# Row maxima 28 tiles ahead instead of 26 in a 16-head attention, and another way of fetching the bias scale before it

## The reference, cut to what matters

```
xn   = layernorm(x)
q, k, v = split(xn @ W_qkv.T)                    # 16 heads of 16, per batch 2048 tokens
core = -dist / max(dist) * 0.1                   # 256 points; dist = pairwise distance of the centres
bias = zeros(N, N); bias[1:257, 1:257] = core
attn = softmax(q @ k.T * scale + bias)
s    = (attn @ v) @ W_proj.T + b_proj + layernorm(xn)
out  = x + s * silu(ffn(xn))
```

## Time and profile before

| what | value |
|---|---|
| median of 3 runs | 2928.17 us |
| profiled execution: its own time | 2928.38 us |
| profiled execution: span of the core | 2926.6 us |
| mean granted TensorE clock | 0.993 |
| PE busy | 2883.0 us (99%) |
| DVE busy | 2336.9 us (80%) |
| ACT busy | 2222.5 us (76%) |
| POOL busy | 1265.3 us (43%) |

### The profile page before, as it was taken

One profiled execution on the slowest core, in us unless ns is written; L12 is line 12 of the kernel. 1 busy time (PEld: TensorE's weight loads), 2 busy tenths in 40 slices (PEclk: granted clock), 3 DMA queues, 4 the chain that ended last, 5 costly groups with the idle time before them and its releaser, 6 DMA issues.

```text
span 2926.6 us, 107289 instructions
## 1 busy us (share of the span) xinstructions
PE 2883.0 (99%) x44160; PEld 2025.9 (69%) x44160; DVE 2336.9 (80%) x4346; ACT 2222.5 (76%) x4251; POOL 1265.3 (43%) x2348
## 2 busy tenths in 40 slices
PE   8899999999999999999999999999999999999998
PEld 4467666655667755767657777777777777777776
DVE  7899999999999999999856776777677677767765
ACT  4599999999999999999966666666666666666664
POOL 5432333333333323332345455555555554555554
PEclk9899999999999999999999999999999999999999
DMA  7631111111111111111121111111111111111110
GB/s 233 211 115 41 49 49 45 43 49 49 41 46 49 49 39 48 49 49 39 44 65 45 36 31 37 40 47 44 30 37 33 47 45 36 31 38 39 47 43 5
DMA packets 157393, 154.78 MB, mean 53 GB/s; under 512 B 17794, under 2 KB 130946, under 8 KB 156930
## 3 DMA queue, kind: packets, MB, share of 16 engines
q1 hardware_dynamic: 156930, 148.15, 16.3%
HBM read 89.37 MB, written 58.72 MB: 51 GB/s over the span
## 4 chain that ended last, share of the span: by engine, by line
PE 95%; DVE 2%; POOL 1%; ACT 1%; issue 1%; SPq 0%; DMA 0%; POOLq 0%; DVEq 0%; ACTq 0%
PE banks L1534 29%; PE banks L1492 15%; PE banks L1460 15%; PE banks L1475 14%; PE banks L1601 4%; PE banks L1549 4%; PE banks L1639 4%; PE banks L1568 3%; PE banks L1616 2%; PE banks L1429 1%; PE banks L1626 1%; DVE pair_max L1145 1%; PE banks L1447 1%; POOL row_max L641 1%; PE banks L1714 0%
## 5 line engine op out<-in xcount | busy, mean ns | idle before, releaser
L1145 DVE TENSOR_REDUCE pair_max<-banks 128x1 f32<-128x1024 f32 x1024 | 1212.4, 1214 | 106.9 <-PE banks L1460 76.4
L919 ACT ACTIVATE probs<-banks 128x512 f32<-128x512 f32 x2048 | 1186.5, 599 | 99.3 <-PE banks L1475 13.1
L1475 PE MATMUL banks<-q_aug,k_aug 98*32 98x512 bf16 x8192 | 845.7, 381 | 0.2
L1460 PE MATMUL banks<-k_aug,q_aug 96*32 96x512 bf16 x8192 | 663.0, 383 | 8.5 <-DVE pair_max L1145 3.8
L1492 PE MATMUL banks<-probs,v_cur 128*32 128x256 f32 x8192 | 655.7, 379 | 2.1 <-POOL probs L635 2.0
L1492 PEld LDWEIGHTS banks<-probs,v_cur 128*32 128x32 f32 x8192 | 319.3, 111 | 144.1 <-issue 2.4
L1460 PEld LDWEIGHTS banks<-k_aug,q_aug 96*32 96x32 bf16 x8192 | 276.8, 97 | 188.2 <-DVE pair_max L1145 60.2
L641 POOL TENSOR_SCALAR row_max<-pair_max 128x1 f32<-128x1 f32 x508 | 139.6, 278 | 611.0 <-DVE pair_max L1145 603.1
L1475 PEld LDWEIGHTS banks<-q_aug,k_aug 98*32 98x32 bf16 x8192 | 287.3, 95 | 150.4 <-ACT probs L919 4.7
L1534 PEld LDWEIGHTS banks<-hnT,w_sb 128*64 128x64 f32 (+1 forms) x5632 | 308.5, 137 | 25.1 <-ACT hnT L998 25.1
L1534 PE MATMUL banks<-hnT,w_sb 128*64 128x128 f32 (+1 forms) x5632 | 323.9, 275 | 0.9 <-ACT hnT L998 0.9
(11 more groups left out here) (143 smaller groups left out, 4020.5 us busy)
## 6 DMA issues: line engine op xcount, KB each, us to landing
acc_scratch<-acc_sb SPq DMA_DIRECT2D x128, 256.0 KB, 2.5
heads_win<-acc_scratch SPq DMA_DIRECT2D x512, 64.0 KB
q_aug<-q_parts SPq DMA_DIRECT2D x192, 64.0 KB, 2.2
k_aug<-k_parts SPq DMA_DIRECT2D x192, 64.0 KB, 2.2
q_parts<-parts SPq DMA_DIRECT2D x16, 384.0 KB, 3.1
k_parts<-parts SPq DMA_DIRECT2D x16, 384.0 KB, 4.1
x_in<-in_x SPq DMA_DIRECT2D x10, 512.0 KB, 4.9
xT_scratch<-xnT SPq DMA_DIRECT2D x8, 512.0 KB, 5.4
```

Of the source, the lines that this page charges most:

```text
L919: nc.scalar.activation(probs[:, step % PRING, :], banks[:, ring(h, step), :], ACT.Exp, scale=SCALE).then_inc(prob_ready, 1)
L1145: nc.vector.tensor_reduce(pair_max[:, group % 2, q, half:half + 1], banks[:, 4 + 2 * (t % 2):6 + 2 * (t % 2), :], AX.XY, ALU.max).then_inc ...
L1460: last = nc.tensor.matmul(banks[m:m + CT, 4 + t % 4, :], q_aug[0:TERM_ROWS, b, q * P + m:q * P + m + CT], k_aug[0:TERM_ROWS, b, kq * BANK: ...
L1475: last = nc.tensor.matmul(banks[m:m + CT, ring(h, step), :], k_aug[0:AUG, b, kb * P + m:kb * P + m + CT], q_aug[0:AUG, b, qc * CHUNK:(qc + ...
```

## The change

`LEAD` goes from KB + 10 to KB + 12, for TensorE and VectorE alike. The maximum over partitions goes by DRAM: SyncE stores one value per partition, waits for it, and loads all 128 into every partition; VectorE reduces them. In chunk 7 VectorE does the distances' sum ahead of `split_rest(c, 0)` and their maximum ahead of `split_rest(c, 2)`. TensorE waits for `v_saved` after the first pair of max tiles instead of ahead of it. The first three score steps stand after 22, 24 and 26 max tiles, where the first stood after 26.

```diff
-LEAD = KB + 10
+LEAD = KB + 12
+EARLY = SRING
@@ sync, behind the loop over chunks
+            sp.wait_ge(dist_red, 1)
+            sp.dma_start(dmax_dram, dmax[:, 0:1]).then_inc(dmax_stored, 16)
+            sp.wait_ge(dmax_stored, 16)
+            sp.dma_start(dmax_all[:], dmax_dram.rearrange("p o -> (p o)").partition_broadcast(P)).then_inc(dmax_in, 16)
             for mb in range(NMB):
                 sp.wait_ge(parts_stored[mb], 16 * (NCHUNK + 1))
             load_aug(0, 1)
@@ gpsimd, chunk 7
-                if not ahead2 and not ahead:
-                    pool.wait_ge(dist_red, 1)
-                    nc.gpsimd.partition_all_reduce(dmax[:, 1:2], dmax[:, 0:1], P, RMAX).then_inc(dist_red, 1)
@@ vector
-                split_rest(c, 0)
-                residual(c, u)
                 if not ahead:
                     dve.wait_ge(dist_step, 3)
                     nc.vector.tensor_tensor(dist[:], dist[:], dtmp[:], ALU.add).then_inc(dist_step, 2)
+                split_rest(c, 0)
+                residual(c, u)
                 split_rest(c, 1)
+                if not ahead:
+                    dve.wait_ge(dist_sqrt, 1)
+                    nc.vector.tensor_reduce(dmax[:, 0:1], dist[:], AX.XY, ALU.max).then_inc(dist_red, 1)
...
-                if not ahead:
-                    dve.wait_ge(dist_sqrt, 1)
-                    nc.vector.tensor_reduce(dmax[:, 0:1], dist[:], AX.XY, ALU.max).then_inc(dist_red, 1)
                 split_rest(c, 3)
@@ vector, behind turn_shift(0, 0)
+            dve.wait_ge(dmax_in, 16)
+            nc.vector.tensor_reduce(dmax[:, 1:2], dmax_all[:], AX.X, ALU.max).then_inc(dist_red, 1)
             dve.wait_ge(dist_red, 2)
@@ tensor
-            pe.wait_ge(v_saved, NCHUNK + 1)
...
-            for t in range(LEAD):
+            for t in range(LEAD - 2 * EARLY):
+                if t == 2:
+                    pe.wait_ge(v_saved, NCHUNK + 1)
                 max_tile(0, t)
             pe.wait_ge(minus_set, 1)
+            for step in range(EARLY):
+                scores_to_exp(0, step)
+                for t in range(LEAD + 2 * (step - EARLY), LEAD + 2 * (step - EARLY) + 2):
+                    max_tile(0, t)
...
-                    if not (ends and step >= STEPS):
+                    if not (ends and step >= STEPS or h == 0 and step < EARLY):
                         scores_to_exp(h, step)
```

More of the change, by code:

```diff
@@ L13 @@
 AX = mybir.AxisListType
-RMAX = bass.bass_isa.ReduceOp.max
 BANK = 512
@@ L95, in build @@
     res_dram = nc.dram_tensor("res_scratch", (T, D), F32, kind="Internal").ap()
+    dmax_dram = nc.dram_tensor("dmax_scratch", (P, 1), F32, kind="Internal").ap()
     acc_dram = nc.dram_tensor("acc_scratch", (B, HEADS, P, N), F32, kind="Internal").ap()
@@ L134, in build @@
         dmax = sb("dmax", [P, 8], F32)
+        dmax_all = sb("dmax_all", [P, P], F32)
         v_all = sb("v_all", [P, T // P, D], F32)
@@ L220, in build @@
         dist_red = sem("dist_red")
+        dmax_stored = sem("dmax_stored")
+        dmax_in = sem("dmax_in")
         dist_scale = sem("dist_scale")
```

## The result

The changed kernel takes 2948.36 us, the median of 6 runs (2946.18 to 2950.89); the kernel before took 2928.25 us in 6 runs beside it. The ratio is 1.0069, interval 1.0056 to 1.0082: slower by 20.1 us, where 15.3 us were forecast. Its profiled execution took 2948.12 us at a span of 2946.3 us and a mean granted clock of 0.994.

A forecast was written before the change was run, and what follows sets the result against it. TensorE was taken to set the pace in the middle of stage 2, VectorE at its start. Start -4.3 and lead +19.6 us: 2928.2 - 4.3 + 19.6 = 2943.5 us, range 2938 to 2955.

The forecast's parts named there:

- The lead: Stage 2, step 75 of 15 heads: TensorE's stall grows from 0.29 to 1.60 us, 15 x 1.31 = +19.6 us.
- the chain: Each head with a next: step 71's weighted call, GpSimd's copy, row maxima, VectorE's turn of group 5's shift; 2.08 us.
- Rival A: Step 75: the hold does not grow with the lead, so only the start counts, 2923.9 us; chance 0.10.
- Rival B, the clock: Stage 2: the 1.6 us stall drops the granted clock, 1.7 us a head, 2956 to 2969 us; chance 0.09.
- Group 1's cover of 0.9 us: Each head: group 1's turn, behind batch 0's bias factors, stays covered, taken as 0; if not, 0 to 4 us.
- The switch of GpSimd's code: Start of stage 2: GpSimd's 5.4 us before the bias factors is the switch back from the reduction's code, and goes.
- rival C: Start of stage 2: GpSimd's 5.4 us stays, the start gains about 0.5 us, total 2947.3 us; chance 0.06.
- The start: Start of stage 2: earlier pairs and bias factors bring pair 20 at about 135.05; together -4.3 us.
- I take the store as landed at 116, the broadcast at 119: Bias scale at the start: SyncE's store and broadcast of the maxima finish then, so VectorE, asking at 119.8, needn't wait.
- My bound of -2.6: The start's smallest gain, -2.6 us, with a late broadcast; the other bound was -5.5.
- SyncE's queue: Start: the wait and two issues put the 12 loads back about 1 us, `phase1_end` 122.2 to 123.2; covered.
- the room above the forecast: Range's upper end, 2955 us: group 1 adds its 4 us and some heads lose the clock.

The follow-up runs named there:

- second run: Kernel before with only the lead changed from 26 to 28, its old start kept: 2950.43 us, ratio 1.0073.
- run 12: Changed kernel with a lead of 30 tiles instead of 28: 2994.65 us, ratio 1.0228.
- run 9: Changed kernel with group 5's maxima ahead of GpSimd's copy and the maximum over partitions by TensorE, plus an unused store of 128 neighbouring 4-byte values: 2918.78 us.
- runs 10 and 11: As run 9, but the unused store writes its values 512 bytes apart, or 128 full rows of 512 bytes: 2918.05 and 2918.45 us.
- runs 5 and 6: Changed kernel with group 5's maxima ahead of GpSimd's copy and the maximum over partitions by TensorE, leads 28 and 26: 2918.68 and 2917.26 us.
- run 7: Changed kernel with the 4-byte store of the maxima issued earlier, behind the first store of the q parts: 2944.94 us, ratio 1.0053.
- run 4: Kernel before (lead 26, old start) with group 5's maxima and shift ahead of GpSimd's copy of the next head's values: 2923.30 us, ratio 0.9983.

## Why the prediction was right, point by point

- **The lead: right in place and size.** Forecast a stall of 1.60 us at step 75, +19.6 us; measured 1.61 us in head 0 and +19.6 us. A head takes 85.2 us instead of 83.9, as forecast. Undoing the lead, setting it alone, and taking the chain away each move the time by what this says. VectorE's wait came out at 2.06 us and not 1.6: before, VectorE had also waited 0.59 us for TensorE ahead of pair 48, slack that I left in; some 0.45 us of it now pass into the wait for the turn. TensorE's stall doesn't depend on it, because the turn's time is set by GpSimd.
- **Rival A is refuted.** Pair 51 does wait for pair 49. Had the hold not grown, the second run would have come out at about 2928 us, and it took 2950.43.
- **Rival B, the clock: not at this stall.** In the profiled execution the changed kernel's clock is 1.00 throughout stage 2 from 132 us on. Behind stalls of 2.90 to 3.05 us (run 12) it fell 12 times of 15, and then cost what the rival said, 1.7 us a head.
- **Group 1's cover of 0.9 us held at lead 28** (15 waits and no more). At lead 30 it was gone, at 0.3 us a head, the price set for it.
- **The switch of GpSimd's code: right; rival C is refuted.** The first bias factor starts at 133.82, 0.14 us behind the memset (133.41 + 0.27), where 5.4 us lay between them before. The first weighted call has no idle time ahead of it.
- **The start: the step that failed is "I take the store as landed at 116, the broadcast at 119".** The store landed at 121.8 and the broadcast at 125.3 (its own 3.4 us were near the 3 us assumed). I had taken 1.9 us from a small load and the queue ahead of it for the rest; that a store of single values could be slower than both was in no row. VectorE reads pair 8 at 126.13 instead of 120.6, 5.5 us late, and pair 20 starts at 140.32 instead of 135.05. So the start gives +0.9 us (+1.3 - 0.4) and not -4.3. My bound of -2.6 was too narrow: it used the longest transfer in my rows, 4.3 us, and the store took 9.8. The other steps of the start hold: first pair 108.97 (forecast 108.8), eight pairs done at 118.65 (118.8). With the maximum by TensorE pair 8 was read at 121.35, near the forecast.
- **SyncE's queue: mis-sized for the same reason.** The 12 loads start 7.1 us later (122.34 against 115.24), not 1 us. ScalarE's table load therefore starts at 128.13 instead of 123.2. Here VectorE was late by as much, so its own price doesn't show. It isn't nothing: in run 9, where only these loads are late, step 64's score comes about 3 us later than in runs 10 and 11 (the granted clock also stays at 0.50 until 136.3 there, against 127.6 and 132.3).

The start came out 5.2 us worse than forecast and the median 4.9 us; the sign rested on the lead, which was sized from one timeline. That the median still lies inside 2938 to 2955 is in part luck: the room above the forecast was meant for group 1 and the clock, neither of which came, and it took up a miss that I had not foreseen. With all three the time would have been near 2960 us.

## What to carry to other kernels

Running one stage further ahead can cost time where something that its consumers wait for does not move along: list, for each buffer that is freed in order, the waits tied to the steps that do not move (here a copy tied to a score step), and see whether the lead eats their slack. Once the slack is gone, the stall of the engine that sets the pace grows by the full shift (1.3 us for each two steps here), and at lead 30 the clock took 1.7 us more in 12 heads of 15. With the wait out of the way, two tiles more ahead gained nothing either (runs 5 and 6). To bring 128 single values into every partition, a diagonal tile and one matmul took under 2 us here and no queue; the store and the broadcast took 13 us and held up the same queue.

## What the runs showed of the hardware that I had not expected

- A store of 128 values of 4 bytes to neighbouring addresses took 9.1 to 10.1 us from issue to landing (in seven kernels), against 3.5 us 512 bytes apart and 3.5 us as full rows. The store queued ahead of it was reported complete only at 121.6 instead of 115.2, and in run 7 the stores behind it waited. In the changed kernel the 16 updates of its semaphore came one after another, from 116.8 to 121.8 us, while the DMA engines' busy share was 0.00:

```profile
118.00:120.00 2.00, 1.54 (x16) 0.14 (x8) 1.48 (x5) 0.00 (x0) 0.26 (x1) 0.50 0.00 0
```

  On such writes the Trainium skill (DMA: Bandwidth & Descriptors, Specifications) says that below 512 bytes the engine does read-modify-write. No run here shows a read. By the times, being below 512 bytes is not enough to be slow: 4-byte writes 512 bytes apart took 3.5 us. That such steps queue on a shared block is my reading; the runs show only the times.
- In the three kernels with PARTITION_ALL_REDUCE, GpSimd's next two-input operation begins 4.2 to 5.4 us after the memset that it waits for: 5.4 us in the kernel before and in run 4, 4.2 us in run 2 (130.03 + 0.27, and 134.50). In the kernels without that reduction it begins 0.1 us after it (133.82 in the changed kernel, 129.18 in run 5). That this is the way back from the reduction's code is my reading. The Trainium skill (GPSIMD Engine Reference, 2.1 Instruction dispatch) prices the first call alone.
- The granted clock stayed at 1.00 behind 15 stalls of 1.6 us and fell to 0.50 (1.2 GHz) behind 12 of 15 stalls of 2.90 to 3.05 us, for 3.4 us each time.
